# Attention maxima: a chained maximum in place of a merging step, and a causal mask multiplied from bf16 tiles

## The reference, cut to what matters

```
scores = jnp.einsum('bhqd,bhkd->bhqk', q, k) / np.sqrt(D_K).astype(np.float32)
causal = jnp.tril(jnp.ones((S, S), dtype=bool))
scores = jnp.where(causal, scores, -jnp.inf)
attn = jax.nn.softmax(scores, axis=-1)
out = jnp.einsum('bhqk,bhkd->bqhd', attn, v).reshape(B, S, D_MODEL)
```

## Time and profile before

| what | value |
|---|---|
| median of 3 runs | 3025.01 us (3016.74 to 3033.07) |
| span of the profiled execution (its own time beside it isn't given) | 3027.5 us |
| TensorE busy | 2895.4 us (96%) |
| VectorE busy | 2179.3 us (72%) |
| ScalarE busy | 1341.6 us (44%) |
| GpSimd busy | 1833.5 us (61%) |
| attention stage | about 605 to 1700 us |
| VectorE, maxima with mask (L247) | 469.3 us in 992 |
| VectorE, plain maxima (L253) | 339.2 us in 496 |
| TensorE, mask products (L1389) | 704 |

### The profile page before, as it was taken

How to read it: one execution, slowest core, us unless ns; L and a number is a source line. 1 busy time by engine, 2 the same in 40 slices (tenths; PEclk the granted TensorE clock), 3 DMA queues, 4 the chain that set the end, 5 groups by cost and what they waited for, 6 DMA issues and landing times.

```text
span 3027.5 us, 49806 instructions
## 1 busy us (share of the span) xinstructions
PE 2895.4 (96%) x16480; PEld 2168.3 (72%) x16480; DVE 2179.3 (72%) x5344; ACT 1341.6 (44%) x2436; POOL 1833.5 (61%) x1077
## 2 busy tenths in 40 slices
PE   8999999999999999999999989999999999989997
PEld 5788888766666666666666677777777787767775
DVE  6555555678787878787877687777777787756664
ACT  2222222156666666666666522233222333226664
POOL 1233222278888888888886256766565666655664
PEclk9999999999999999999999999999999999999998
DMA  7655555756655665566555333332322322238996
GB/s 240 211 187 201 187 180 180 233 114 136 137 124 115 138 138 121 115 139 140 119 117 160 107 97 93 94 112 74 103 79 93 102 85 81 73 107 222 239 245 118
DMA packets 281948, 420.53 MB, mean 139 GB/s; under 512 B 48463, under 2 KB 132687, under 8 KB 281742
## 3 DMA queue, kind: packets, MB, share of 16 engines
q1 hardware_dynamic: 259214, 384.22, 44.9%
q0 software_dynamic: 22528, 33.72, 5.8%
HBM read 263.38 MB, written 153.01 MB: 138 GB/s over the span
## 4 chain that ended last, share of the span: by engine, by line
PE 53%; DVE 14%; POOL 14%; issue 8%; ACT 4%; DMA 4%; another core or an unknown queue 2%; DVEq 1%; POOLq 0%; SPq 0%; ACTq 0%
PE qkv_ps_m L840 12%; PE ffn_ps_m L2191 11%; POOL att_gathered L1105 6%; PE qkv_ps_m L844 6%; POOL att_pt L1098 5%; PE att_ps_o L1330 5%; PE att_ps_p L1386 4%; PE att_ps_s L1304 4%; DMA out<-exp_y,exp_tok_add 2%; PE exp_ps_u L1607 2%; PE exp_ps_y L1623 1%; PE att_ps_s L1361 1%; DVE ffn_att L147 1%; DVE ffn_x L149 1%
## 5 line engine op out<-in xcount | busy, mean ns | idle before, releaser
L247 DVE CUSTOM_DVE_ANT_0 att_ps_s<-att_ps_s,att_causal 128x512 f32<-128x512 f32 (+1 forms) x992 | 469.3, 502 | 175.5 <-PE att_ps_s L1304 171.3
L1166 ACT ACTIVATE att_pt<-att_ps_p 128x512 f32<-128x512 f32 (+1 forms) x1024 | 524.5, 589 | 143.6 <-PE att_ps_p L1389 110.2
L1304 PE MATMUL att_ps_s<-att_ks,att_qs 96*128 96x512 f32 x1488 | 513.4, 373 | 2.2 <-DVE att_lower L253 0.6
L1386 PE MATMUL att_ps_p<-att_qs,att_ks 98*128 98x512 f32 (+3 forms) x1536 | 498.5, 364 | 9.3 <-ACT att_pt L1166 8.0
L1098 POOL TENSOR_TENSOR att_pt<-att_pt 128x1024 f32<-128x1024 f32 (+2 forms) x153 | 331.1, 2164 | 166.6 <-PE att_ps_o L1330 144.8
L1105 POOL TENSOR_TENSOR att_gathered<-att_gathered,att_pt 128x2048 f32<-128x2048 f32 (+1 forms) x92 | 388.1, 4218 | 7.2
L1912 POOL DMA_INDIRECT slot_info<-ffn_info,ffn_slot x256 | 275.9, 1078 | 119.3 <-issue 76.5
L253 DVE TENSOR_REDUCE att_lower<-att_ps_s 128x1 f32<-128x512 f32 x496 | 339.2, 684 | 7.4 <-PE att_ps_s L1304 7.4
L1386 PEld LDWEIGHTS att_ps_p<-att_qs,att_ks 98*128 98x128 f32 x1536 | 272.6, 191 | 82.1 <-issue 34.7
L1304 PEld LDWEIGHTS att_ps_s<-att_ks,att_qs 96*128 96x128 f32 x1488 | 275.7, 191 | 73.3 <-DVE att_rowmax L247 27.7
L577 POOL TENSOR_TENSOR qkv_x<-qkv_x,qkv_mod 128x512 f32<-128x512 f32 x60 | 83.4, 1391 | 371.5 <-DVE qkv_x L671 371.5
(11 more groups left out here) (311 smaller groups left out, 6718.8 us busy)
## 6 DMA issues: line engine op xcount, KB each, us to landing
att_qs<-qk_parts SPq DMA_DIRECT2D x96, 512.0 KB, 6.8
att_ks<-qk_parts SPq DMA_DIRECT2D x96, 512.0 KB, 12.7
qk_parts<-qkv_out_hi SPq DMA_DIRECT2D x128, 256.0 KB, 2.2
qk_parts<-qkv_out_lo SPq DMA_DIRECT2D x128, 256.0 KB, 2.4
qkv_x<-x SPq DMA_DIRECT2D x16, 1024.0 KB, 5.6
v_rows<-qkv_out_v SPq DMA_DIRECT2D x64, 256.0 KB, 2.3
att_vs<-v_rows SPq DMA_DIRECT2D x32, 512.0 KB, 16.1
o_parts<-att_o SPq DMA_DIRECT2D x64, 256.0 KB, 7.9
```

Source lines behind the costliest of these rows:

```text
L247: dve.tensor_tensor_reduce(part, part, self.causal[:, UNIT - (c1 - c0):UNIT], scale=1.0, scalar=MASKED, op0=ALU.add, op1=ALU.max, accum_ou ...
L1166: act.activation(tile(c)[:, h, col:UNIT], ps_p[(NPROB * prev.g + n) % NP][:, col:UNIT], ACT.Exp, scale=float(HD) ** -0.5).then_inc(exp_don ...
L1304: pe.matmul(bank("s", cur.g, i)[:, 0:c1 - c0], qs[cur.slot][0:STACK, h, t * P:(t + 1) * P], ks[cur.slot][0:STACK, h, c0:c1], start=True, s ...
L1386: last = pe.matmul(part[:, i * (UNIT - col):(i + 1) * (UNIT - col)], ks[prev.slot][:, h + i, kt * P:(kt + 1) * P], qs[prev.slot][:, h + i, ...
```

## The change

The list of pieces is reordered: for each pair of tiles the lower piece of tile 7-a, the single piece of tile a, then the upper piece of tile 7-a. The upper piece's fused instruction starts its maximum from the lower piece's result, one value per partition in SBUF, instead of MASKED, and waits for it on `max_done`, two pieces back. The merging `tensor_tensor` and its wait are gone, and the transpose waits for 48 increments instead of 49. The two tiles of the mask product are bf16 instead of f32r; an unused tile fills the space that they leave, so that all others keep their addresses. GpSimd writes both tiles once, with the same copies as before (L591, L602).

```
-ORDER = [(h, t) for a in range(KT // 2) for h in range(GH) for t in (KT - 1 - a, a)]
-PIECES = [(h, t, c0, min(c0 + UNIT, (t + 1) * P)) for h, t in ORDER for c0 in range(0, (t + 1) * P, UNIT)]
+PIECES = [piece for a in range(KT // 2) for h in range(GH)
+          for piece in ((h, KT - 1 - a, 0, UNIT), (h, a, 0, (a + 1) * P), (h, KT - 1 - a, UNIT, (KT - a) * P))]
 N1 = len(PIECES)
-NMAX = N1 + 1
+NMAX = N1
...
-        self.ident_r = s.sb("ident_r", [P, P], F32R)
-        self.mask_k = s.sb("mask_k", [P, GH, P], F32R)
+        self.ident_r = s.sb("ident_r", [P, P], BF16)
+        self.mask_k = s.sb("mask_k", [P, GH, P], BF16)
+        s.sb("beside_masks", [P, (GH + 1) * P], BF16)
...
             dve.sem_inc(self.mark, 1)
+            below = MASKED
+            if c0:
+                low = h * LOW + t - LOW
+                below = under[:, low:low + 1]
+                dve.wait_ge(self.max_done, CREDIT + NMAX * g + i - 1)
             dve.tensor_tensor_reduce(part, part, self.causal[:, UNIT - (c1 - c0):UNIT], scale=1.0,
-                                     scalar=MASKED, op0=ALU.add, op1=ALU.max,
+                                     scalar=below, op0=ALU.add, op1=ALU.max,
...
     def negate(self, dve, g, bank):
 
-        rows, under = self.rowmax[g % 2], self.lower[g % 2]
-        dve.wait_ge(self.max_done, CREDIT + NMAX * g + N1)
-        dve.sem_inc(self.mark, 1)
-        upper = rows[:, :].rearrange("p (h t) -> p h t", t=KT)[:, :, LOW:KT]
-        dve.tensor_tensor(upper, upper, under[:, :].rearrange("p (h t) -> p h t", t=LOW), ALU.max).then_inc(self.max_done, 1)
         dve.wait_ge(self.mt_done, CREDIT + g + 1)
```

## The result

The changed kernel takes 3030.57 us (median of 20 runs, 3021.90 to 3045.62), the kernel before 3017.99 us beside it on the same chip (20 runs): ratio 1.0049, 95% interval [1.0035, 1.0064] (worked out from the single runs; the two medians alone, 12.6 us apart, give 1.0042). Later, on another chip, the same pair gave 1.0026 [1.0002, 1.0050]. The profiled spans are 3034.2 us after and 3027.5 before, 6.7 us apart. So it is slower, at the edge of what a measurement of this kernel tells, and inside the range 3014 to 3058. The traces account for 6.7 us; what makes up the rest of the 12.6 no run here shows.

What follows compares the result with a forecast made beforehand. TensorE's order was taken to bound the attention stage, VectorE and ScalarE stalling it. -0.03 + 0.05 + 0.23 + 0.13 = +0.38 us a group, times 31 = +11.8, with -0.5 beforehand, together +11: median 3036, range 3014 to 3058.

Steps and rivals of the forecast that it cites:

- the turn: At the transpose of the maxima, without the merging step: -0.03 us a group, as ScalarE's exponentials limit the gain.
- the masks' loads: bf16 mask loads wait for the f32 matmul ahead: +0.017 us for each of 16, +0.012 for four, -0.038 for two.
- the operand's price: Each of 16 upper pieces a group costs VectorE 0.055 us more with a start value per partition; bounds 0 and 0.06.
- the second stretch: Second stretch of scores, limited by VectorE: four upper pieces +0.22, order +0.05 and -0.04, masks 0; +0.23 us a group.
- the third stretch: Third stretch, last score matmul waits for a 512-wide maximum: +0.13 us a group, masks 0; bounds 0 and +0.35.
- rival (a): The transpose's whole 0.84 us wait is TensorE time and ScalarE doesn't eat it: -13 us, 3012; 8%.
- The first stretch: First stretch of scores, behind ScalarE's limit: masks 0.024 - 0.038 + 0.068 = +0.05 us a group, chained maxima 0.
- (c): The bf16 mask load is hidden under the f32 matmul ahead as well: +8 us, 3033; 10%.
- (d): Type changes drain TensorE both ways, so the f32 load behind a mask waits until it has streamed: 3070 to 3089; 9%.
- (b): The pointer operand is free in the chained maximum's instruction: +2 us, 3027; 20%.
- (e): The pointer instruction waits for GpSimd like the merging step, up to 2 us for each of 16: over 3100; 3%.
- The group scored beforehand: The group scored in the stage before: a transpose no longer waits for the merging step there, taken at -0.5 us.

Runs made afterwards that it cites:

- Experiment 9: The kernel of experiment 8 with its merging step as one reduction over pairs instead of a maximum of two tiles: ratio 0.9976 to the kernel before.
- experiment 8: The kernel before with bf16 only for the masks of 256 and 512 columns: ratio 1.0003 to the kernel before.
- experiment 4: The kernel after with masks in f32r and the merging step kept beside the chained maxima: ratio 1.0020 to the kernel before.
- 3: The kernel before with only the new order of pieces; separate maxima, merging step and f32r masks stay: ratio 1.0018 to the kernel before.
- experiment 6: The kernel before with a pointer to a column of constants as the start of all 32 masked maxima of a group: ratio 1.0056 to the kernel before.
- the chain alone: The kernel after with its masks back in f32r (new order, chained maxima, no merging step): ratio 1.0044 to the kernel before.
- experiment 7: The kernel after with the old order of pieces and f32r masks, each chained maximum straight behind its forerunner: ratio 1.0156 to the kernel before.

## Why the prediction was right, and where it was not

The time came out at +12.6 us between the medians where +11 was forecast, with the sign right. That nearness is in part luck: the traces show +6.7, and of the +0.38 us a group 0.23 came. The mechanisms named for the turn and for the masks' loads held; the operand's price in the second stretch was three times too high, and the third stretch, put too low by 0.035, made up for little of it.

**The turn (-0.03).** Counted from the last column sums to the end of A, the kernels before and after take 7.107 and 7.117 us (medians of the whole way). Experiment 9 against experiment 8 has the turn by itself: from there to the end of A 0.016 less, in the period 0.019 less. So -0.02 came, near the forecast's -0.03 and for the reason that it gave: the transpose came 0.088 earlier, ScalarE's first exponential 0.018 and the next 0.034. The stall was 0.09, inside its 0.06 to 0.2. (The sets of column sums lie 0.43 us apart, as the prediction uses, not the 0.41 that it writes; and the 25.1 us of rows 2 are in 28 waits, so rival (a) would be 0.90 and not 0.84 us each.) Rival (a), the whole of that wait, is refuted by experiments 4 and 9.

**The first stretch (+0.05).** Taken with the turn +0.02 was forecast and 0.010 came. On this way the masks alone make +0.035 (7.107 to 7.142), the order alone +0.037 (to 7.144), though the forecast had the order at 0 there; the order with the chain and without the step makes nothing (7.105), and no run parts these. With the order alone TensorE's loads for the second pass wait for ScalarE twice as often as before (605 to 1640 us; before, then the order alone):

```profile
PEld att_ps_p L1386 <- ACT att_pt L1166: 23.2, 61, 0.6
```
```profile
PEld att_ps_p L1386 <- ACT att_pt L1166: 35.8, 120, 0.7
```

In A the timeline shows one such wait of 0.17 us before, and two, 0.17 and 0.19, with the order alone. The order has the narrow piece second, so TensorE probably reaches a bank too soon that ScalarE still reads; that this is the cost is argued and not shown.

**The second stretch (+0.23): the step that failed.** "The bank awaited last hangs on four upper pieces: 4 x 0.055 = +0.22". B grew by 0.076, of which the operand has 0.066 (experiment 4 against 3). The duration was right: in experiment 4 chained maxima are 0.05 to 0.07 us longer than the others of their width (602 against 555 ns at 384 columns, 354 against 287 at 128), at 512 columns:

```profile
L252 DVE CUSTOM_DVE_ANT_0 att_ps_s<-att_ps_s,att_causal,att_lower 128x512 f32<-128x512 f32 x124 | 92.1, 743 | 0.9 <-PE att_ps_s L1309 0.6 <-issue 0.2
L252 DVE CUSTOM_DVE_ANT_0 att_ps_s<-att_ps_s,att_causal 128x512 f32<-128x512 f32 x123 | 85.0, 691 | 1.6 <-PE att_ps_s L1309 0.4
```

Four times that duration was not. The stretch on VectorE with the order alone, then after (reads of the accumulator left out):

```profile
777.75 0.60 DVE L247 CUSTOM_DVE_ANT_0 att_ps_s<-att_ps_s,att_causal 128x384 f32<-128x384 f32 x1
778.26 0.69 DVE L253 TENSOR_REDUCE att_lower<-att_ps_s 128x1 f32<-128x512 f32 x1
...
779.20 0.60 DVE L247 CUSTOM_DVE_ANT_0 att_ps_s<-att_ps_s,att_causal 128x384 f32<-128x384 f32 x1
```
```profile
784.32 0.62 DVE L253 CUSTOM_DVE_ANT_0 att_ps_s<-att_ps_s,att_causal,att_lower 128x384 f32<-128x384 f32 x1
784.85 0.69 DVE L259 TENSOR_REDUCE att_lower<-att_ps_s 128x1 f32<-128x512 f32 x1
...
785.79 0.62 DVE L253 CUSTOM_DVE_ANT_0 att_ps_s<-att_ps_s,att_causal,att_lower 128x384 f32<-128x384 f32 x1
```

From the 384-wide piece to the reduction pass 0.516 us without the pointer and 0.538 with it (medians). Elsewhere in the kernel before the same step with the constant takes 0.483 in two cases of five, and in experiment 6, with the pointer, 0.538 in those as well. So in this stretch 0.03 us stood between the two instructions that the profile doesn't book as idle time, and the pointer filled them first; what they are no run shows. Three such pieces lie in the stretch before its last bank is awaited; the fourth stands behind the reciprocal, and from its start to the reduction's both kernels have 0.46. So 3 x 0.022 = 0.07. The order's 0.05 and -0.04 hold as a sum: with the order alone B is unchanged. In experiment 6, where another masked maximum follows the operand directly, the full 0.060 is paid.

**The third stretch (+0.13).** +0.165. The awaited piece is the 512-wide one, as forecast: its maximum starts at 768.73, its accumulator is read by 769.48, and the last score load follows.

```profile
768.73 0.69 DVE L253 CUSTOM_DVE_ANT_0 att_ps_s<-att_ps_s,att_causal 128x512 f32<-128x512 f32 x1
769.34 0.14 DVE L253 DVE_READ_ACCUMULATOR2_ANT att_rowmax<- 128x1 f32 x1
769.53 0.19 PEld L1305 LDWEIGHTS att_ps_s<-att_ks,att_qs 96*128 96x128 f32 x1 [0.48 <-DVE att_rowmax L253]
```

Its terms were order +0.051, operand +0.046, masks +0.065 (the rest, 0.003, is the step's absence). In the forecast the operand had 0.11, the order what is left of 0.40 after 0.2 to 0.25 and 0.16, so about 0.02, and the masks 0: the operand was put too high, the order too low, and the masks' zero was wrong. The near agreement of the sum, 0.13 and 0.165, is luck. The masks had been put at 0, "VectorE decides the end". It does, but VectorE is fed by TensorE in the first half of C: against the chain alone, VectorE's maxima of the kernel after start 0.007 us later at 23.2 us behind the transpose, 0.054 at 24.7 and 0.074 at 25.4, and keep this to the end. In B, where VectorE has no gap, the masks added 0.015. So 0 was nearly right for B and wrong for C.

**The masks' loads.** As forecast: in the kernel after the bf16 load starts with the end of the matmul ahead, the next f32 load with the mask's own matmul, beside the earlier trace rows:

```profile
745.09 0.40 PE L1387 MATMUL att_ps_p<-att_qs,att_ks 98*128 98x512 f32 x1
745.33 0.10 PEld L1390 LDWEIGHTS att_ps_p<-att_mask_k,att_ident_r 128*128 128x128 bf16 x1 [0.28 <-issue]
745.33 0.23 PE L1390 MATMUL att_ps_p<-att_mask_k,att_ident_r 128*128 128x128 bf16 x1
745.34 0.20 PEld L1305 LDWEIGHTS att_ps_s<-att_ks,att_qs 96*128 96x128 f32 x1
```

From the product through its narrow mask to the next product, with a 128-column score behind, it is 0.43 us here (745.09 to 745.52) and 0.40 before (744.77 to 745.17); the medians of such sequences differ by 0.017 to 0.020 (forecast 0.017), and each 512-column mask gave back 0.053 (forecast 0.038). The Trainium skill, "TensorE: Matmul & The Clock Gate", section "Part 2: What happens when you issue a matmul", has the next load run under the present matmul; for a bf16 load behind an f32 stream the trace again does not agree (81.2 us of idleness by issue in 380 loads). Rivals (c) and (d) fall with this, (b) with experiment 6, and (e) with the pointer pieces' 0.05 to 0.07: the longest of them took 0.76 us, none waited for GpSimd.

**The group scored beforehand (-0.5).** The first transpose stands at 638.9 in both traces: 0. In the forecast's sum the second stretch had 0.154 x 31 = 4.8 us too much and the turn with the first stretch 0.010 x 31 = 0.3; the third had 0.035 x 31 = 1.1 and this group 0.5 too little. That leads from 11.3 to 7.8, where the median period gives 7.0 and the way from the first transpose to the last 6.2.

## What to carry to other kernels

A wait removed at one place is worth what the next engine in line has not already taken: count from the last event that both kernels share (here the column sums) to the next common end, not to the instruction that waited. Read what an operand adds from the instruction's start to its successor's start, once for each kind of successor, and count only those ahead of the event that is awaited; its added duration times its count gave three times too much here. And an engine that decides a stretch's end may still be fed by another in that stretch's first half: a cost there reaches the end in full.

## What the hardware showed

A 128x16 maximum of two SBUF tiles takes 0.16 us at the least and 2.39 in the median, ending with GpSimd's addition; as a reduction of one tile of pairs it takes 0.19 in the midst of such an addition. The Trainium skill, "GPSIMD Engine Reference", in the table at its head, puts the contention on instructions with two SBUF inputs; the pair of runs agrees. A maximum that takes its start from the instruction just ahead of it starts some 0.12 us later than it would otherwise (experiment 7: 0.72 against 0.60). A wait of the profile's list can be a name and no cost: 0.84 us by the step in experiment 4, 0.84 by issue without it.
